# Reordering the second token group of a float32 language-model tower: sines inside the selection, biases as rows of the products, means as extra columns

## The chip, the cores and the metric

One NeuronCore of a Trainium2 chip runs the whole kernel in one launch. The metric is device time in microseconds, the median of several runs. The kernel before took 168.65 us (three runs, 168.17 to 169.03).

## The reference

Four sequences of 512 tokens, 64 channels, float32. Three layers follow each other:

```
# token layer
weighted = where(mask & ~eye, rel_dist, 0)
h = [atom_embed[ids], (weighted @ neighbor_embed[ids]) * w_rd] @ w1 + b1
h = silu(layernorm(h) * gamma + beta) @ w2 + b2
# attention layer, on x = layernorm(h)
ao     = gelu([x, pp] @ hop_w1 + hop_b1) @ hop_w2 + hop_b2       # 4 heads of 32 phases + 1 width
center = tanh(ao[:32]) * pi ; width = sigmoid(ao[32]) * 2 + 0.1
q      = cos/sin(pp + center + offsets), weighted by exp(-d^2 / 2 width^2), summed over 5 offsets
key_ph = tanh(x @ cpe_w + cpe_b) * pi ; values = x @ ve_w + ve_b
gate   = sigmoid(gelu(x @ sg_w1 + sg_b1) @ sg_w2 + sg_b2)
st_ph  = tanh(gelu([x, ctx/pos] @ ksk_w1 + ksk_b1) @ ksk_w2 + ksk_b2) * pi
combined = causal sums of (content, values * gate) against (cos, sin) of these phases
h = h + x + (layernorm(combined) * ln_g + ln_b) @ out_w + out_b
# experts, on x = layernorm(h): the best 2 of 8
h = h + sum over the 2 chosen experts of gelu(x @ W1[e] + b1[e]) @ W2[e] + b2[e]
```

## The kernel before, in words

**Tiles.** The four sequences form two groups of two. A group has 4 chunks of 128 tokens for each of its 2 sequences, so most tiles are 128 x 512, with tokens on the partitions, or channels of both sequences on them. PSUM is eight banks of 128 x 512 float32 (`bank[0]` to `bank[7]`), reused by hand.

**Stages.** Every engine has a function of the same name for each stage: `token(g)` (T), `project(g)` (P), `queries(g)` (Q), `chunks(g)` (C), `weights` (W) and `experts(g)` (X). Each is a generator, cut into parts by `yield`. `ORDER` (L83) is one list such as `P0 Q0 P1`; `follow` runs on each engine the next part of the named stage and group. The list is thus the program order of all engines together, each engine with its own parts of it; the instructions of an engine run strictly in that order. A part is written here as P1[2]: third part of `project` for group 1. Between engines there are only semaphores, `S[...]`.

**The parts that matter here.**

- T: TensorE multiplies by the centred second weight into bank 5 (L676), then by a two-column mean weight into bank 7 (L681). VectorE adds the bias to get h (L1160), takes the variance of ScalarE's squares, an inverse root in seven small operations (`rsqrt`, L1017), and writes x (L1168) and the means (L1170).
- P[0]: TensorE transposes x, ScalarE copies it out (L433); VectorE scans it (L1178). P[1]: the hop product (L703) and the position product (L704) into bank 1, the gate product (L707), two joint products of values, content and key phases (L712); ScalarE's two Gelus; VectorE adds the joints' biases (L1184). P[2]: the small width and gate products z (L727, L731), the storage product (L734, L736), joints 2 and 3; VectorE adds z's biases (L1190, L1192); ScalarE's third Gelu (L447) and the tanh of z. P[3]: centre products (L744), VectorE adds their bias into `t_c` (L1206), ScalarE takes the tanh in place (L458). P[4]: storage phase products (L756), their bias on VectorE (L1210), their tanh, and the gate's running sums (L762, L764, read at L1213).
- Q, on VectorE: Q[0] widths, Q[1] base angles (L1229), Q[2] sums over the five offsets, Q[3] an inverse root, the argument of the arctangent and the magnitude, Q[4] phases added to the angles (L1274), Q[5] the turn into range (L1280), Q[6] magnitude times sine and cosine (L1288), Q[7] sums over the heads into `feat` (L1295, L1299). ScalarE beside it: exponent, absolute value, key sines (L478), arctangent, rounding (L489), query sines (L494 to L500).
- C: C[0] TensorE transposes the keys (L783), C[1] the queries (L796), C[2] first scores, C[3] to C[5] a chunk each (scores L807 and L812, state, outputs L838 to L845), C[6] last outputs, C[7] variance and output products (L863, L869) and the output's means by two columns (L873), C[8] h3. On VectorE C[0] of group 0 also runs `weight_parts` (L1124), which centres the output weight and takes the low halves of expert weights.
- X[1]: VectorE's norm and split of the expert input; X[3]: selection of two experts, 16 small operations, ending in `mask_set`; X[4]: TensorE transposes the split with the mask (L926); from X[5] on one hidden product pair each (L944, L945), a Gelu (L574), and every second time four back products (L960).
- `spin_products(n, bank)` (L588) multiplies a constant tile n times and uses the result nowhere.

Two lines tell how an engine waits and why an order counts:

```
pe.wait_ge(S["q_sum"], 2 * g + 2)      # C[1]: query transposes
dve.wait_ge(S["gate_mm"], g + 1)       # P[4]: gate sums
```

After the group-1 query sums the list alternates C1 and X0, then X1 and X0, then X1 alone.

Of the kernel before, what the change touches and what calls it, by code (L numbers as in the profile page):

```python
# [45 lines left out]
P = 128  # L46
# [16 lines left out]
MASK_ROWS = 32  # L63
BIAS_AT, MASK_AT = D, D + MASK_ROWS
# [13 lines left out]
        ("hop2w_bd", P, 2 * H), ("hop_b2w", P, H)]  # L78
# [4 lines left out]
ORDER = ("T0 T0 T0 T0 T1 T1 T0 T0 T1 T0 T1 P0 P0 T1 P0 T1 Q0 P0 T1 W0 P0 Q0 P1 Q0 Q0 P1 Q0 Q0 Q0 Q0 P1 C0 P1 "  # L83
         "P1 C0 Q1 C0 Q1 C0 C0 Q1 C0 C0 Q1 C0 C0 X0 Q1 X0 Q1 X0 X0 C1 Q1 X0 X0 X0 X0 Q1 C1 X0 C1 X0 C1 X0 C1 X0 C1 X0 "
         "C1 X0 C1 X0 C1 X0 X1 X0 X0 X1 X0 X0 X1 X0 X0 X1 X0 X0 X1 X1 X1 X1 X1 X0 X1 X1 X1 X1 X1 X1 "
# [20 lines left out]
def tower(nc, ids, dist, mask, early, folded, late, ffn, mrows, out):  # L106
# [4 lines left out]
    with ExitStack() as ctx:  # L111
# [14 lines left out]
        def view(tile, table):  # L126
# [8 lines left out]
        w2c_bd = sb("w2c_bd", [P, P])  # L135
        w2_mean = sb("w2_mean", [P, NH_])
        b2c_rows = sb("b2c_rows", [P, D])
        shift = sb("shift", [P, 2])
        out_mean = sb("out_mean", [P, NH_])
# [8 lines left out]
        outw_g = sb("outw_g", [P, P])  # L148
# [85 lines left out]
        xp1 = [sb(f"xp1_{g}", [P, 8 * P], F32R) for g in range(NG)]  # L234
        xp2 = [sb(f"xp2_{g}", [P, 8 * P], F32R) for g in range(NG)]
# [20 lines left out]
            dist_masked h1_mm h1_copied h1t_mm h1_sq h1_norm hn_mm f_set h2_mm h_set h_mean_mm h_mean_set x_sq x_set  # L256
            trig_abs trig_set kang_set fold_mm fold_set fused_set
            xt_mm xt_set cx_set hop_mm hop_set sg_mm sg_set vk_mm vk_set z_mm zg_set tg_set ksk_mm ksk_set
# [7 lines left out]
        hid_bank = (0, 1, 3)  # L266
        x_bank = (0, 4)
# [15 lines left out]
        def b3(i):  # L283
            return bank[i][:, :].rearrange("p (t d) -> p t d", d=D)

# [104 lines left out]
        def _(act):  # L390
            def token(g):
# [19 lines left out]
                if g:  # L411
                    act.wait_ge(S["h_mean_mm"], g)
# [14 lines left out]
            def project(g):  # L427
# [14 lines left out]
                yield  # L442
# [4 lines left out]
                nc.scalar.activation(ksk_g[:, :], bank[2][:, :], ACT.Gelu,  # L447
                                     bias=ksk_bias[:, :]).then_inc(S["ksk_set"], 1)
                act.wait_ge(S["zg_set"], g + 1)
                nc.scalar.activation(tg[:, g], zg[:, g], ACT.Tanh, scale=0.5).then_inc(S["tg_set"], 1)  # L450
# [4 lines left out]
                for k in range(2):  # L455
                    act.wait_ge(S["center_set"], 2 * g + k + 1)
                    half = flat(t_c[:, g, 4 * k:4 * k + 4])
                    nc.scalar.activation(half, half, ACT.Tanh).then_inc(S["center_tanh"], 1)  # L458
                yield
                act.wait_ge(S["st_set"], g + 1)  # L460
# [124 lines left out]
        def _(pe):  # L585
# [14 lines left out]
            def token(g):  # L600
# [72 lines left out]
                if g:  # L673
                    pe.wait_ge(S["h_set"], g)
# [837 lines left out]
```

## Time and profile before

| | |
|---|---|
| median of three runs | 168.65 us (168.17 to 169.03) |
| the profiled execution | 169.19 us |
| its span in the trace | 167.4 us |
| mean granted TensorE clock | 0.959 |
| TensorE, VectorE, ScalarE busy | 149.0, 116.6, 81.8 us |
| the chain that ended last | TensorE 54%, VectorE 32%, ScalarE 6%, issue 6% |

The span is the time between the first and the last instruction in the trace; the rest of the execution lies around it. A busy TensorE need not be at its peak, since matmuls are pipelined and filling products count as busy. The granted clock is the share of 2.4 GHz: 1.00, or 0.50 for 1.2 GHz.

### The profile page before, as it was taken

How to read it: one execution, taken by the hardware profiler on the slowest of the kernel's cores; microseconds unless marked ns; L12 is line 12 of the kernel's file. 1: busy time of each engine (PE TensorE's matmuls, PEld its weight loads, DVE VectorE, ACT ScalarE, POOL GpSimd, SP SyncE). 2: the span in 40 equal slices, each digit the busy share in tenths (PEclk: the TensorE clock that was granted, in tenths of full speed). 3: DMA queues.
4: the chain of work that ended last, by engine and by line, in shares of the span. 5: the costliest groups of instructions: out<-in, count | busy, mean ns of one | idle time of the engine just before them, and what ended most of it. 6: DMA issues, size and time to landing. Idle time of an engine off the chain costs nothing.

```text
span 167.4 us, 2358 instructions
## 1 busy us (share of the span) xinstructions
PE 149.0 (89%) x806; PEld 88.4 (53%) x812; DVE 116.6 (70%) x344; ACT 81.8 (49%) x137; POOL 8.8 (5%) x38
## 2 busy tenths in 40 slices
PE   5899999999999988649699997786999999899991
PEld 1382565537693336429586752463665764553530
DVE  6999879975798989499859899993434788031202
ACT  3001151469389637962970232897224366545721
POOL 5403100140000000000000000000000000000000
PEclk9999999999999999956858999999999999999999
DMA  4899950300000000000000000000000000002011
GB/s 119 321 427 427 417 205 6 125 0 0 0 4 0 0 0 2 0 2 0 0 4 0 0 4 0 0 2 0 0 4 0 0 4 0 0 0 63 0 31 31
DMA packets 3778, 9.21 MB, mean 55 GB/s; under 512 B 2356, under 2 KB 2484, under 8 KB 3256
## 3 DMA queue, kind: packets, MB, share of 16 engines
q1 hardware_dynamic: 3768, 9.08, 14.6%
q8 instruction: 6, 0.10, 0.2%
q14 instruction: 4, 0.03, 0.1%
HBM read 8.55 MB, written 0.52 MB: 54 GB/s over the span
## 4 chain that ended last, share of the span: by engine, by line
PE 54%; DVE 32%; ACT 6%; issue 6%; POOL 0%; DVEq 0%; POOLq 0%; ACTq 0%
PE bank L960 9%; PE bank L944 6%; PE bank L646 5%; PE bank L945 4%; PE bank L624 3%; PE bank L807 2%; DVE invpos L1035 2%; PE bank L637 2%; DVE q_sc L1295 2%; DVE q_sc L1288 2%; PE bank L712 1%; PE bank L812 1%; PE bank L603 1%; PE bank L676 1%; DVE dist_sb L1274 1%
## 5 line engine op out<-in xcount | busy, mean ns | idle before, releaser
L590 PE MATMUL bank<-spin 128*128 128x512 bf16 x92 | 24.5, 398 | 5.2 <-POOL spin L328 2.0
L574 ACT ACTIVATE hid<-bank 128x512 f32<-128x512 f32 x32 | 17.9, 602 | 21.5 <-PE bank L945 21.4
L590 PEld LDWEIGHTS bank<-spin 128*128 128x128 bf16 x98 | 9.2, 104 | 15.8 <-issue 2.7
L960 PE MATMUL bank<-hid,ffn_sb 128*64 128x512 f32 x64 | 16.4, 612 | 0.0
L944 PE MATMUL bank<-xp,w1hi 128*128 128x512 f32 x32 | 14.6, 455 | 0.9 <-ACT xp L554 0.9
L1406 DVE TENSOR_TENSOR h<-bank,h 128x256 f32<-128x256 f32 (+1 forms) x5 | 1.8, 367 | 18.6 <-PE bank L971 12.8
L1313 DVE TENSOR_TENSOR dist_sb<-bank,fold_sb 128x256 f32<-128x256 f32 x16 | 6.0, 419 | 10.4 <-PE bank L812 9.8
L945 PE MATMUL bank<-xp,w1lo 128*128 128x512 f32 x32 | 12.6, 395 | 0.0
L944 PEld LDWEIGHTS bank<-xp,w1hi 128*128 128x128 f32 x32 | 6.0, 188 | 7.9 <-ACT hid L574 3.6
L646 PE MATMUL bank<-dist_sb,neigh 128*64 128x512 f32 x32 | 9.3, 699 | 0.0
L1085 DVE TENSOR_TENSOR dist_sb<-dist_sb,mask_in 128x1024 f32<-128x1024 f32 x8 | 9.2, 1218 | 0.0
L744 PE MATMUL bank<-late_sb,proj 128*128 128x256 f32 x16 | 5.7, 519 | 3.8 <-ACT proj L447 3.8
L807 PE MATMUL bank<-dist_sb 64*128 64x256 f32 x16 | 6.7, 502 | 1.5 <-ACT dist_sb L516 0.9
L395 ACT COPY neigh<-bank 128x512 f32<-128x512 f32 x2 | 1.2, 585 | 11.6 <-PE bank L624 11.6
L812 PE MATMUL bank<-dist_sb 64*128 64x128 f32 x32 | 6.8, 340 | 0.0
L1288 DVE TENSOR_TENSOR q_sc<-q_sc,mag 128x512 f32<-128x512 f32 x8 | 5.1, 687 | 2.4 <-ACT q_sc L497 2.4
L960 PEld LDWEIGHTS bank<-hid,ffn_sb 128*64 128x64 f32 x64 | 3.4, 135 | 6.3 <-issue 3.9
L744 PEld LDWEIGHTS bank<-late_sb,proj 128*128 128x128 f32 x16 | 3.8, 257 | 5.0 <-ACT proj L447 4.1
L945 PEld LDWEIGHTS bank<-xp,w1lo 128*128 128x128 f32 x32 | 6.1, 189 | 0.4
L646 PEld LDWEIGHTS bank<-dist_sb,neigh 128*64 128x64 f32 x32 | 3.1, 165 | 6.0 <-issue 4.9
L624 PEld LDWEIGHTS bank<-tables,onehot 100*128 100x128 f32 x32 | 5.4, 261 | 0.8 <-DVE tables L1056 0.8
L624 PE MATMUL bank<-tables,onehot 100*128 100x64 f32 x32 | 5.6, 348 | 0.0
(270 smaller groups left out, 318.3 us busy)
## 6 DMA issues: line engine op xcount, KB each, us to landing
dist_sb<-in_dist SPq DMA_DIRECT2D x4, 1024.0 KB, 11.2
mask_in<-in_mask SPq DMA_DIRECT2D x2, 512.0 KB, 8.1
fold_sb<-in_folded SPq DMA_DIRECT2D x1, 998.0 KB, 11.0
ffn_sb<-in_ffn SPq DMA_DIRECT2D x1, 816.0 KB, 17.4
late_sb<-in_late SPq DMA_DIRECT2D x1, 728.5 KB, 15.9
mask_in<-in_mrows SPq DMA_DIRECT2D x1, 512.0 KB, 3.1
out<-h SPq DMA_DIRECT2D x8, 64.0 KB, 1.7
early_sb<-in_early SPq DMA_DIRECT2D x1, 167.0 KB, 2.4
```

Of the source, the lines that this page charges most:

```text
L574: nc.scalar.activation(hid[:, at % HB], bank[hid_bank[at % 3]][:, :], ACT.Gelu).then_inc(S["hid_set"], 1)
L590: nc.tensor.matmul(bank[i][:, :], spin[:, 0:P], spin[:, :], start=True, stop=True)
L624: mm = nc.tensor.matmul(b3(5 if g == 0 else 7)[:, t], onehot[:, at:at + P], tables[:, D:2 * D], start=True, stop=True)
L646: mm = nc.tensor.matmul(rows(f), neigh[:, b, j], dist_sb[:, b, j], start=False, stop=(j == NC - 1), skip_group_check=True)
L744: mm = nc.tensor.matmul(bank[i][:, c * 256:(c + 1) * 256], hop_g[:, (2 * k + c) * P:(2 * k + c + 1) * P], K["hop2c_bd"], start=True, stop= ...
L807: nc.tensor.matmul(bank[4][:, 0:2 * P], k_t[lo, c, 0], q_t[lo, c].rearrange("p f i -> p (f i)"), start=True, stop=True).then_inc(S["s_mm"], 1)
L812: mm = nc.tensor.matmul(bank[5][:, f * P:(f + 1) * P], k_t[hi, c, f], q_t[hi, c, f], start=True, stop=True)
L944: nc.tensor.matmul(o, w1hi[:, e * HID:(e + 1) * HID], xp1[g][:, toks], start=True, stop=False)
L945: nc.tensor.matmul(o, w1lo[:, e * HID:(e + 1) * HID], xp2[g][:, toks], start=False, stop=True).then_inc(S["hid_mm"], 1)
L960: mm = nc.tensor.matmul(bank[2][j * D:(j + 1) * D, :], K["e_w2"][:, (e + j) * D:(e + j + 1) * D], hid[:, (at + j) % HB], start=False, stop ...
L1085: nc.vector.tensor_tensor(dist_sb[:, b, rows], dist_sb[:, b, rows], mask_sb[:, b, rows], ALU.mult).then_inc(S["dist_masked"], 1)
L1288: nc.vector.tensor_tensor(q3, q3, bc(mag[:, 16 * k:16 * k + 16], PH), ALU.mult).then_inc(S[done], 1)
```

## The change

1. **Order.** In the list, C0[0] (group 0's key transposes) moves ahead of Q0[4], and P1[1] behind Q0[5]: so the second group's joints on VectorE, its Gelus on ScalarE and its products on TensorE come after the first group's angles and sines. P1[2], P1[3] and P1[4] are interleaved with C0[2], C0[3] and C0[4]. Q1[0] to Q1[2] follow between C0[4] and C0[7]. Q1[3] comes after X0[2] instead of ahead of C0[7], C1[0] right after it, then Q1[4] and Q1[5], and only then X0[3], the selection, and Q1[6].
2. **Biases of group 1.** z, centre and storage phase biases come as an extra product at the head of each group of products: 64 rows of ones against 64 rows that hold the bias split into a high and a low float32r part (row 0 and row 32; the rest zero). ScalarE makes the high part and the ones in W, VectorE the low part (`bias_parts`) in P1[0]. ScalarE's tanh then reads the bank itself; VectorE's three additions go for group 1. Group 0 keeps them.
3. **Means as columns.** The token layer's and the output's mean weights become columns 129 and 130 of the same weight tile; chunks 0 and 1 go to bank 5, 2 and 3 to bank 7, and the separate mean products go. VectorE reads h, the scaled output and the means in two halves.
4. **Front of P[1].** The position product goes ahead of the wait for x; three filling products go. For group 1 the storage product and its Gelu move into P1[1], in bank 6.
5. **Weight parts** move from C0[0] to C0[1].
6. **Filling products** get new places and waits.

```
@@ ORDER
+ORDER = ("T0 T0 T0 T0 T1 T1 T0 T0 T1 T0 T1 P0 P0 T1 P0 T1 Q0 P0 T1 W0 P0 Q0 P1 Q0 Q0 C0 Q0 Q0 P1 Q0 Q0 C0 P1 "
+         "C0 P1 C0 P1 C0 Q1 C0 Q1 C0 Q1 C0 C0 X0 X0 X0 Q1 C1 Q1 Q1 X0 Q1 X0 X0 X0 X0 Q1 C1 X0 C1 X0 C1 X0 C1 "
...
@@ ScalarE, project
-                yield
+                if g == 0:
+                    yield
                 act.wait_ge(S["ksk_mm"], g + 1)
...
+                nc.scalar.activation(tg[:, g], bank[1][:, 0:40] if g else zg[:, g], ACT.Tanh, scale=0.5).then_inc(S["tg_set"], 1)
...
+                    nc.scalar.activation(half, bank[2 + k][:, :] if g else half, ACT.Tanh).then_inc(S["center_tanh"], 1)
@@ ScalarE, weights
+                nc.scalar.copy(b_rows[:, :], K["bias_rows"]).then_inc(S["b_hi"], 1)
+                nc.scalar.copy(b_ones[:, :], ones[0:2 * MASK_ROWS, 0:P]).then_inc(S["b_ones_set"], 1)
@@ TensorE, token
+                    mm = nc.tensor.matmul(with_mean(c // 2)[:, c % 2], f_t[:, c * P:(c + 1) * P], w2_ext[:, :],
...
-                    mm = nc.tensor.matmul(bank[7][:, c * NH_:(c + 1) * NH_], f_t[:, c * P:(c + 1) * P], w2_mean[:, :],
-                                          start=True, stop=True)
@@ TensorE, project
-                spin_products(3, 2)
+                nc.tensor.matmul(bank[1][:, :], K["hop1p"], K["pp_T"], start=True, stop=False)
                 pe.wait_ge(S["xt_set"], g + 1)
...
                 joint(0, 3)
                 joint(1, 0)
                 if g:
                     pe.wait_ge(S["h1_norm"], NG)
+                    storage()
+                    pe.wait_ge(S["h_mean_set"], NG)
+                    spin_products(4, 7)
+                    pe.wait_ge(S["phi_set"], 1)
+                    spin_products(5, 7)
+                    pe.wait_ge(S["th_sum"], 2)
+                    spin_products(5, 7)
+                    pe.wait_ge(S["th_set"], 2)
+                    spin_products(3, 7)
+                    last_joints()
+                    spin_products(3, 7)
+                    pe.wait_ge(S["cos_set"], 1)
+                    spin_products(3, 7)
+                    pe.wait_ge(S["cos_set"], 2)
+                    spin_products(4, 7)
+                yield
+                if g:
+                    pe.wait_ge(S["hop_set"], 2)
+                    pe.wait_ge(S["b_ones_set"], 1)
+                    pe.wait_ge(S["b_lo"], 1)
+                    nc.tensor.matmul(bank[1][:, 0:40], b_ones[:, :], b_rows[:, Z_AT:ST_AT], start=True, stop=False, skip_group_check=True)
...
                 def center(k, i):
+                    if g:
+                        nc.tensor.matmul(bank[i][:, :], b_ones[:, :],
+                                         b_rows[:, CENTER_AT:NB].unsqueeze(1).broadcast_to([2 * MASK_ROWS, 4, P]),
+                                         start=True, stop=False, skip_group_check=True)
@@ TensorE, chunks
+                if g == 0:
+                    pe.wait_ge(S["h_mean_set"], NG)
+                    spin_products(4, 2)
+                    pe.wait_ge(S["kph_abs_set"], 1)
+                    spin_products(5, 2)
+                    pe.wait_ge(S["k_feat"], 1)
+                    spin_products(5, 2)
...
                 yield
+                if g == 0:
+                    pe.wait_ge(S["ksk_set"], NG)
+                    pe.wait_ge(S["q_cos"], 2)
+                    spin_products(2, 7)
                 pe.wait_ge(S["q_sum"], 2 * g + 2)
@@ TensorE, experts, X0[3] and X0[5]
+                    spin_products(3, 2)
+                    pe.wait_ge(S["at_arg"], 2)
+                    spin_products(6, 2)
+                    pe.wait_ge(S["phi_set"], 2)
+                    spin_products(5, 2)
+                    pe.wait_ge(S["th_sum"], 4)
+                    spin_products(6, 2)
+                    pe.wait_ge(S["th_set"], 4)
                     spin_products(6, 2)
                     pe.wait_ge(S["first_best"], 1)
-                    spin_products(6, 2)
+                    spin_products(7, 2)
...
+                    spin_products(3, 2)
@@ VectorE
+            def bias_parts():
+                dve.wait_ge(S["b_hi"], 1)
+                low = slice(MASK_ROWS, 2 * MASK_ROWS)
+                nc.vector.tensor_tensor(b_rows[low, :], K["bias_rows"][low, :], b_rows[low, :].bitcast(F32),
+                                        ALU.subtract).then_inc(S["b_lo"], 1)
...
+                for n in range(2):
+                    dve.wait_ge(S["attn_mm"], 2 * g + n + 1)
+                    factor = st_c[:, 4 * n:4 * n + 4].rearrange("p (c f) -> p c f", f=NH_).unsqueeze(3).broadcast_to([P, 2, NH_, D])
+                    ins = nc.vector.tensor_tensor(comb[:, 2 * n:2 * n + 2], rows_of(n), factor, ALU.mult)
```

## Rows read from the trace of the kernel before

**Rows 1.** Windows, all engines: from:to, length, busy (instructions) by engine, granted clock:

```profile
98.00:110.00 12.00, 9.84 (x57) 5.62 (x57) 11.01 (x38) 7.12 (x13) 0.00 (x0) 1.00 0.01 1
115.00:128.00 13.00, 13.00 (x110) 7.74 (x110) 4.90 (x13) 3.96 (x7) 0.00 (x0) 1.00 0.01 1
```

**Rows 2.** Windows of TensorE alone, then granted clock, DMA share, GB/s:

```profile
35.10:37.21 2.11, 2.11 (x4) 1.00 0.00 0
39.83:41.70 1.87, 1.87 (x19) 1.00 0.00 0
45.45:47.22 1.77, 1.77 (x11) 1.00 0.00 0
48.03:49.95 1.92, 1.92 (x18) 1.00 0.00 0
73.51:78.65 5.14, 5.14 (x16) 0.50 0.01 2
78.70:82.05 3.35, 2.41 (x24) 1.00 0.00 0
82.05:88.85 6.80, 6.23 (x49) 0.50 0.01 2
115.92:116.35 0.43, 0.43 (x3) 1.00 0.00 0
122.03:123.71 1.68, 1.68 (x26) 1.00 0.04 10
```

**Rows 3.** Timeline, 45 to 60 us: start, length, engine, line, operation, tiles:

```profile
45.69 0.69 DVE L1160 TENSOR_TENSOR h<-bank,b2c_rows 128x512 f32<-128x512 f32 x1 [0.32 <-PE bank L676]
...
50.15 0.24 ACT L537 CAST eb<-ffn_sb 32x64 fp32r<-32x64 f32 x1
...
52.60 1.22 DVE L1229 TENSOR_TENSOR dist_sb<-dist_sb,half_turn 128x1024 f32<-128x1024 f32 x1
...
54.34 1.23 DVE L1178 TENSOR_TENSOR_SCAN proj<-ones,proj 128x512 f32<-128x512 f32 x1 [0.53 <-issue]
```

**Rows 4.** Timeline, 60 to 75 us, first group's query sines and sums:

```profile
67.27 1.28 ACT L497 ACT_TABLE_LOAD   x1
...
70.75 0.70 ACT L500 ACTIVATE q_sc<-thn,half_pi 128x512 f32<-128x512 f32 x1
...
74.09 0.49 DVE L1299 TENSOR_TENSOR feat<-q_sc 128x128 f32<-128x128 f32 x2
```

**Rows 5.** Windows of VectorE alone, one block of its order each:

```profile
56.21:58.48 2.27, 2.09 (x10) 1.00 0.00 0
75.60:78.22 2.62, 2.45 (x9) 0.50 0.00 0
80.43:81.78 1.35, 1.21 (x7) 1.00 0.00 0
91.13:95.28 4.15, 3.70 (x19) 1.00 0.00 0
95.28:98.55 3.27, 2.93 (x13) 1.00 0.00 0
98.55:100.64 2.09, 1.95 (x7) 1.00 0.04 8
100.64:104.58 3.94, 3.60 (x13) 1.00 0.00 0
105.78:109.49 3.71, 3.23 (x17) 1.00 0.00 0
109.49:114.37 4.88, 4.81 (x13) 1.00 0.01 2
```

**Rows 6.** Timeline, 90 to 100 us, ScalarE's square of the outputs:

```profile
93.16 0.60 ACT L527 ACTIVATE sq_c<-bank 128x512 f32<-128x512 f32 x1 [6.13 <-PE bank L845]
```

**Rows 7.** The chain that ended last, in order of time: start, length, what:

```profile
114.43 1.09 PE bank L796 x8
...
131.21 0.79 PE bank L873 x8
```

More of the change, by code:

```diff
@@ L679, in token @@
                 yield
-                for c in range(NC):
-                    mm = nc.tensor.matmul(bank[7][:, c * NH_:(c + 1) * NH_], f_t[:, c * P:(c + 1) * P], w2_mean[:, :],
-                                          start=True, stop=True)
-                mm.then_inc(S["h_mean_mm"], 1)
                 yield
@@ L713, in joint, with storage, last_joints @@
                                      stop=True).then_inc(S["vk_mm"], 1)
+                def storage():
+                    i = ksk_bank[g]
+                    nc.tensor.matmul(bank[i][:, :], K["ksk1x_bd"], x_t[:, :], start=True, stop=False)
+                    pe.wait_ge(S["cx_set"], g + 1)
+                    nc.tensor.matmul(bank[i][:, :], wk_bd[:, :], cx[:, :], start=False, stop=True).then_inc(S["ksk_mm"], 1)
+                def last_joints():
+                    for c, i in ((2, 3), (3, 0)):
+                        pe.wait_ge(S["vk_set"], NC * g + c - 1)
+                        joint(c, i)
                 joint(0, 3)
                 joint(1, 0)
+                if g:
+                    pe.wait_ge(S["h1_norm"], NG)
+                    storage()
[13 more added lines that the diff above has]
+                    spin_products(4, 7)
                 yield
                 if g:
[L719 to L724 removed]
+                    pe.wait_ge(S["hop_set"], 2)
+                    pe.wait_ge(S["b_ones_set"], 1)
+                    pe.wait_ge(S["b_lo"], 1)
+                    nc.tensor.matmul(bank[1][:, 0:40], b_ones[:, :], b_rows[:, Z_AT:ST_AT], start=True, stop=False, skip_group_check=True)
                 pe.wait_ge(S["hop_set"], g + 1)
@@ L868, in chunks @@
                 for c in range(NC):
-                    mm = nc.tensor.matmul(bank[5][:, c * P:(c + 1) * P], cc_t[:, c * P:(c + 1) * P], outw_g[:, :],
+                    mm = nc.tensor.matmul(with_mean(c // 2)[:, c % 2], cc_t[:, c * P:(c + 1) * P], outw_ext[:, :],
                                           start=True, stop=True)
-                mm.then_inc(S["attn_mm"], 1)
-                for c in range(NC):
-                    mm = nc.tensor.matmul(bank[7][:, c * NH_:(c + 1) * NH_], cc_t[:, c * P:(c + 1) * P], out_mean[:, :],
-                                          start=True, stop=True)
-                mm.then_inc(S["attn_mm"], 1)
+                    if c % 2:
+                        mm.then_inc(S["attn_mm"], 1)
                 yield
@@ L1168, in token @@
                 nc.vector.tensor_tensor(v8(x[:, g]), v8(h[:, g]), bc(st_r[:, :], D), ALU.mult).then_inc(S["x_set"], 1)
-                dve.wait_ge(S["h_mean_mm"], g + 1)
-                nc.vector.tensor_copy(h_mean[:, g], bank[7][:, 0:8]).then_inc(S["h_mean_set"], 1)
+                for n in range(2):
+                    ins = nc.vector.tensor_copy(h_mean[:, g, 4 * n:4 * n + 4].rearrange("p (c f) -> p c f", f=NH_), means_of(n))
+                ins.then_inc(S["h_mean_set"], 1)
                 yield
```

149 lines of the change are left out of this document (91 added, 58 removed).

## Prediction

> **What bounds the kernel now.** I read four views in this order: the page's forty slices, for where each engine is full and where TensorE's clock falls; the chain that ended last, for who sets the end; the timeline from 20 to 128 us, to lay each engine's order beside the others; windows over single blocks, for prices. A block below is written as in the order: P1[2] is the third part of project for the second group.
>
> From 114.43 on the chain is TensorE, without a gap until 143.5: it begins with the second group's query transposes [rows 7], and TensorE is busy 13.00 of 13 us there [rows 1]. What ends there is therefore set by when those transposes start, plus TensorE work taken out behind them. They start 0.06 us after the second group's query sums end on VectorE, at 114.37 [rows 5, 7]. Before that VectorE carries the chain: busy 11.01 of 12 us between 98 and 110 [rows 1]. So the question is how early VectorE ends the query sums of group 1. TensorE's half clock, 71.85 to 78.65 and 82.05 to 88.85 [rows 2], matters where VectorE waits for its products.
>
> **The change, step by step.** I keep the clock of the profiled execution.
>
> *Front end.* The first group's position product moves ahead of the copy of x it used to follow, and three filling products go. TensorE's transposes of x end about 34.25; position and x products (2.11 together [rows 2]) then end at 36.4 instead of 37.3: 0.9 early, on a stretch in which TensorE is the path to the second group's h. h starts at 45.69 now [rows 3], then at 44.8. Splitting h into two halves over two banks and the means into two copies costs some 0.07 and 0.1. The eight mean products that go cost what the second group's do, 0.79 [rows 7], beside VectorE work here: nothing.
>
> *Before the first queries.* ScalarE gets two casts, of 64x200 and 64x128. The nearest row is 32x64 at 0.24 [rows 3]; below I put 0.2 each, above 0.35 each, and take 0.5 in all. That delays the copy of x that starts the scan, which moves from 54.34 [rows 3] to 53.75 only. The new low part of the biases (0.3) runs while VectorE waits for that copy.
>
> *First group's queries.* At this point the second group's joints, 0.88, no longer stand in front of the angles, so th_sum starts near 63.0 instead of 64.35. The Gelus move behind the sines, so the table load between the absolute value and the first sine, 1.28 at 67.27, goes too. The last cosine, which ended at 71.45 (70.75 plus 0.70), ends at 68.75, and the query sums, which ended at 74.58 [rows 4], end at 71.9: 2.7 earlier. If the load still came, 1.3 of it would be lost. TensorE's new waits (for the turn, the sines, the last Gelu) hold up the last joints and the z products queued behind them, and nobody needs those before 74.5: VectorE stands in the query sums and the weight parts until then.
>
> The Trainium skill (ScalarE: Activation LUTs, "What ACT_TABLE_LOAD costs") budgets 2.66 us for each switch, a load of 1.28 and a drain of 1.38. The row has the load at 1.28, and the first sine starts 0.01 behind it, so the drain isn't in this trace. By the page's figure the sums would end 1.4 earlier still, near 70.5.
>
> *What is late next.* ScalarE needs a load and three Gelus after the last cosine (1.28 plus 1.9): to 72.0, and TensorE waits for the last of them, then runs two filling products: 72.45. From there its queue holds, at full clock and by the windows unless said [rows 2]: query transposes 1.09 [rows 7]; the 16 small z products 1.87; first scores 0.6; centre products 1.89 (the eight take 1.77 and a tail); a chunk 1.68; storage phase and gate products 1.92; a chunk 1.68; a chunk with three filling products 2.3; filling and last outputs 1.3: 14.4 us. The four bias products are new. By the nearest row, 512 columns of the same type at 0.43, they cost at most 1.7; below, a third of that and nothing if weights load beside others. I take 1.0. The outputs end at 72.45 + 15.4 = 87.8, against 93.1 now (the square that waits for them starts at 93.16 [rows 6]).
>
> The weight parts, 2.62 [rows 5], run from 71.9 to 74.5 beside the transposes; their cover is TensorE's z products, which VectorE awaits until 76. Were it gone they would cost 2.6. VectorE no longer adds the second group's biases (0.4 for z, 1.2 for centres, 0.4 for storage phases), but it idles while TensorE works: it waits at the gate sums until 82.5. What it saves there is not on the path.
>
> *From the outputs to the query sums of group 1.* Square, variance products and the first read take 2.2 now (93.1 to 95.28) and again: 89.95. VectorE has by then, after its second chunk at 84.1, the exponents' start 1.35, the base angles 1.22, the exponent sums 2.27 [rows 3, 5] and a masked chunk of 1.0: 89.95 too, a tie. Then, all on VectorE [rows 5]: variance to h3 and means 3.27, plus 0.1 for the halves, to 93.3; it waits 0.35 for ScalarE's square; norm and split 3.94, to 97.6; magnitude chain 4.15, now here, to 101.75; phases and their sums 2.09, to 103.85; a wait of 0.35 and the turn, 1.20 (between the rows ending 104.58 and starting 105.78), to 105.4; selection 3.71, to 109.1; products and sums 4.88, to 114.0. The sines need 3.4 after 104.9, so they end at 108.3, under the selection. Today's order has the same blocks and ends at 114.37. So five microseconds won at the outputs are nearly all spent again: today the magnitude chain fills VectorE's waits in the chunk stage, afterwards it stands in the open. What is left is 0.4.
>
> *Behind the transposes.* The second group's eight mean products, 0.79 at 131.21 [rows 7], go from a stretch where TensorE is the path; two more columns per product cost nothing visible. If ScalarE, which must do h3's square before its next Gelu, becomes late, none of it is kept; I take 0.8. The early scores and expert transposes (ready 7 us sooner) win nothing, because the mask ends at 109.1 and hidden products queue behind the query transposes anyway. The added 102 KB of biases ride in the fourth load, needed at 34.5 long after all loads have landed: nothing.
>
> Sum: 0.4 + 0.8 = 1.2. The profiled execution took 169.19 (span 167.40 and 1.79 around), so 168.0 in its terms; it lay 0.54 above the median of the three timed runs, 168.65, so I forecast 167.4 for the median. With all unknown costs at their good ends (biases 0.5, casts 0.3) it is 166.7; at their bad ends 168.2.
>
> **Rivals.**
>
> *The clock falls in the chunk stage (slower).* Now it fell once after TensorE had stood idle from 69.7, and once at 82.05, after a stretch in which it was busy 2.41 of 3.35 us, mostly with gate products of a few columns, and idle for 0.95 [rows 2]. The new queue puts z products of 8 and 2 columns and gate products of 8 and 6 in a row with scores. For it: such products alone preceded the second fall. Against: the new filling products leave no idle microsecond from 57 to 72.5, and small products from 48 to 50 fell between dense ones at full clock. Each half-clock stretch lasted 6.80 us [rows 2]; one of them over this full queue loses 3.4 us of work, and VectorE has no slack behind it: 167.4 + 3.4 = 170.8. It decides as soon as such a stretch begins between 73 and 84.
> The Trainium skill (TensorE: Matmul & The Clock Gate, "Part 1: The HAM clock gate") has half clock as the default that activity lifts; by that rule a queue kept full with tiny products may still count as quiet. The trace agrees in kind, with 0.50 granted at 82.05.
>
> *Everything is given back (no change).* The sines end only 0.8 under the selection and VectorE ties with TensorE at 89.95; half a microsecond late at two of these, or ScalarE eating the 0.8 around h3, and the transposes start at 114.4 to 115. For it: VectorE's work is the same. Against: the turn and sines have slack on both sides. Time: 168.65, give or take 0.4.
>
> *TensorE's stretch is shorter than its parts (much faster).* If weight loads run ahead and the bias products hide, VectorE's wait at the gate sums shrinks. VectorE's own work from 71.9 on adds up to some 37.4 us, so it could end at 109.3 at the earliest, 5 us before now. Half of the 4.7 us of waits gone gives 167.4 - 2.3 = 165.1. Against: the block prices are starts to starts at full clock, with overlap already in them.
>
> **How the numbers follow.** Forecast 0.46; given back 0.22; much faster 0.16; clock falls 0.16. From about 0.5% this kernel's measurement can tell a change: below 167.8 is faster, above 169.5 slower. Of the forecast four fifths lie below 167.8 (0.37), of the no-change case a small part (0.02): with the fast rival 0.55. Slower is the clock case: 0.16. The rest is 0.29. The likeliest case's own range is 166.7 to 168.2. Cutting half the fast rival and most of the clock case gives 165.2 to 169.8.
>
> **What would show it.** Right: the load before the first sines of group 0 gone and query sums end near 71.9; clock at 1.00 from 70 to 90; VectorE waiting for gate sums near 82; first outputs done near 88; second group's sines inside the selection; transposes near 114.0 and the stretch behind them 0.8 shorter. Wrong: a stretch at 0.50 between 73 and 90; sums of group 0 later than 73; the transposes before 113 or after 115, which means that a VectorE wait I placed is elsewhere.

## The result and the profile after

| | before | changed |
|---|---|---|
| median | 169.25 us (20 runs, 168.14 to 170.36) | 168.41 us (20 runs, 167.25 to 172.09) |
| the profiled execution | 169.19 us, span 167.4 | 168.35 us, span 166.6 |
| mean granted TensorE clock in it | 0.959 | 1.00 |
| TensorE, VectorE, ScalarE busy | 149.0, 116.6, 81.8 us | 152.4, 115.8, 79.7 us |

The ratio of changed to before is 0.9926, with an interval from 0.9898 to 0.9953. Of the 168.65 us on which the forecast was made that is 1.25 us, so 167.4. A few executions of the changed kernel (four of 20, near 172.0 us), and of most variants below, ran 3 to 9 us longer than their siblings; the ratios leave them out. The two profiled executions differ by 0.84 us, less than the ratio's 1.25.

The page of the changed kernel, three of its rows in forty slices. VectorE's thin place lies around the twentieth slice, and TensorE's granted clock does not fall in this execution (it fell twice in that of the kernel before [rows 2]).

```profile
PE   5899999899997799989999997896999999899991
...
DVE  6999879977699989993397899893424788131202
...
PEclk9999999999999999999999999999999999999999
```

ScalarE's timeline, 65 to 71 us, answers to [rows 4]: start, length, engine, line, operation. No table load stands before the sines, and the last cosine ends at 68.4, where it ended at 71.45. The load is now behind the sines, for the three Gelus.

```profile
64.96 0.63 ACT L521 ACTIVATE thn<-dist_sb 128x512 f32<-128x512 f32 x1 [0.21 <-DVE dist_sb L1375]
...
67.67 0.71 ACT L527 ACTIVATE q_sc<-thn,half_pi 128x512 f32<-128x512 f32 x1
68.40 1.28 ACT L452 ACT_TABLE_LOAD   x1
...
70.85 0.67 ACT L462 ACTIVATE proj<-bank,ksk_bias 128x512 f32<-128x512 f32 x1
```

VectorE's timeline, 71 to 92 us; in brackets its idle time and what ended it. The query sums end at 71.5, and then VectorE stands still five times for TensorE, 5.9 us in all, before the variance of the outputs (L1437).

```profile
71.01 0.49 DVE L1394 TENSOR_TENSOR feat<-q_sc 128x128 f32<-128x128 f32 x2
...
75.82 0.76 DVE L1408 TENSOR_TENSOR dist_sb<-bank,fold_sb 128x256 f32<-128x256 f32 x2 [0.90 <-PE bank L877]
...
79.22 0.76 DVE L1408 TENSOR_TENSOR dist_sb<-bank,fold_sb 128x256 f32<-128x256 f32 x2 [1.85 <-PE bank L882]
...
82.25 0.17 DVE L1308 COPY gsum<-bank 128x8 f32<-128x8 f32 x1 [2.08 <-PE bank L823]
82.88 0.76 DVE L1408 TENSOR_TENSOR dist_sb<-bank,fold_sb 128x256 f32<-128x256 f32 x2 [0.46 <-PE bank L882]
...
89.91 0.17 DVE L1437 TENSOR_SCALAR rs_v<-bank 128x8 f32<-128x8 f32 x1 [0.62 <-PE bank L933]
```

TensorE in windows, and its timeline. It is full, filling products included, from 57 to 70 us, stands idle for 0.81 before the first query transposes, and is full again from these to the last output of the first group (16.03 us, at full clock). Two groups of three filling products (L619) stand in front of the third and fourth outputs; in the chain that ended last they take 0.75 us each.

```profile
57.00:70.00 13.00, 13.00 (x50) 1.00 0.00 1
72.02:88.05 16.03, 16.03 (x146) 1.00 0.00 1
```

```profile
71.58 0.60 PE L619 MATMUL bank<-spin 128*128 128x512 bf16 x2 [0.81 <-ACT proj L462]
...
84.86 0.82 PE L619 MATMUL bank<-spin 128*128 128x512 bf16 x3
...
86.42 0.82 PE L619 MATMUL bank<-spin 128*128 128x512 bf16 x3
```

The chain that ended last, in order of time, answers to [rows 7]: the transposes start at 114.09 instead of 114.43. Behind them the chain now leaves TensorE once, for VectorE's scaled output and h3 (L1444, L1447), and then, as before, goes through ScalarE's copies (L593, L583) to the hidden products.

```profile
114.09 1.09 PE bank L866 x8
...
131.86 0.42 DVE dist_sb L1444
132.30 0.70 DVE h L1447
133.05 0.66 PE bank L960 x4
...
142.66 0.59 ACT proj L593
143.25 0.58 ACT xp L583
...
144.08 0.47 PE bank L1020
```

Of the 0.8 us by which the span is shorter, 0.34 is won at the transposes and 0.53 between them and the last block of hidden products (L1020, 144.08; before 144.95).

### The profile page after: what moved, and what is told of

Its sections match the earlier page's. It is cut to its first block, busy times and chain, and to the rows that moved or that the text cites. A ratio compares the mean times of both kernels' runs of the same rounds, so it can differ in the third digit from the quotient of the medians.

```text
span 166.6 us, 2404 instructions
## 1 busy us (share of the span) xinstructions
PE 152.4 (91%) x829; PEld 85.3 (51%) x829; DVE 115.8 (70%) x348; ACT 79.7 (48%) x137; POOL 8.8 (5%) x38
## 4 chain that ended last, share of the span: by engine, by line
PE 53%; DVE 32%; issue 6%; ACT 6%; POOL 0%; DVEq 0%; POOLq 0%; ACTq 0%
PE bank L1036 9%; PE bank L1020 5%; PE bank L1021 4%; PE bank L675 3%; PE bank L653 2%; DVE dist_sb L1161 2%; PE bank L619 2%; DVE invpos L1111 2%; PE bank L877 2%; DVE rs_v L1107 2%; PE bank L738 1%; PE bank L797 1%; PE bank L933 1%; PE bank L882 1%; PE bank L908 1%
## 5 line engine op out<-in xcount | busy, mean ns | idle before, releaser
L619 PE MATMUL bank<-spin 128*128 128x512 bf16 x143 | 36.4, 392 | 6.3 <-POOL spin L342 2.0
L619 PEld LDWEIGHTS bank<-spin 128*128 128x128 bf16 x143 | 13.0, 100 | 25.2 <-issue 4.1
L1020 PE MATMUL bank<-xp,w1hi 128*128 128x512 f32 x32 | 14.7, 458 | 0.4 <-ACT xp L583 0.4
L1508 DVE TENSOR_TENSOR h<-bank,h 128x256 f32<-128x256 f32 (+1 forms) x5 | 1.8, 367 | 18.2 <-PE bank L1047 12.3
L1020 PEld LDWEIGHTS bank<-xp,w1hi 128*128 128x128 f32 x32 | 6.0, 188 | 7.3 <-ACT hid L603 3.6
L882 PE MATMUL bank<-dist_sb 64*128 64x128 f32 x32 | 5.7, 297 | 0.0
L877 PE MATMUL bank<-dist_sb 64*128 64x256 f32 x16 | 5.5, 427 | 0.0
L1107 DVE TENSOR_REDUCE rs_v<-sq 128x8 f32<-128x520 f32 x6 | 4.1, 691 | 1.9 <-ACT sq L422 1.3
L738 PE MATMUL bank<-fold_sb,proj 128*128 128x320 f32 x16 | 5.2, 445 | 0.0
```

Source lines behind the costliest of these rows:

```text
L619: nc.tensor.matmul(bank[i][:, :], spin[:, 0:P], spin[:, :], start=True, stop=True)
L738: nc.tensor.matmul(bank[i][:, 0:VK], x_t[:, c * P:(c + 1) * P], K["vk_bd"], start=True, stop=True).then_inc(S["vk_mm"], 1)
L877: nc.tensor.matmul(bank[4][:, 0:2 * P], k_t[lo, c, 0], q_t[lo, c].rearrange("p f i -> p (f i)"), start=True, stop=True).then_inc(S["s_mm"], 1)
L882: mm = nc.tensor.matmul(bank[5][:, f * P:(f + 1) * P], k_t[hi, c, f], q_t[hi, c, f], start=True, stop=True)
L1020: nc.tensor.matmul(o, w1hi[:, e * HID:(e + 1) * HID], xp1[g][:, toks], start=True, stop=False)
L1107: link(nc.vector.tensor_reduce(rs_v[:, 0:8], squares[:, :, :], AX_X, ALU.add))
```

## Experiments

Each was run beside the kernel before on the same chip; ratios are to it. Edits are shown against the changed kernel, from experiment 10 on against the experiment in front; parts are left out where a line says so in words. In the first set the changed kernel, run again, had 0.9908 (0.9881 to 0.9935), median 168.13 us.

**1. The changed kernel again.** 

> The changed kernel itself, for a base on the same chip. My theory and every rival expect the ratio of the first measurement, 0.993, within its interval. The lists of runs so far have the changed kernel at a clock of 1.00 near 168.4 and at 0.979 near 167.4, and a few at 172.0; I expect the same three kinds of run again, the last by a half-clock stretch in the chunk stage.

It gave 0.9908, 1.6 us gained where the first measurement had 1.25; the intervals overlap.

**2. The second group's old order around the selection.**

```
 ORDER, from Q1[2] to Q1[6]
-Q1[2] C0[7] C0[8] X0[0] X0[1] X0[2] Q1[3] C1[0] Q1[4] Q1[5] X0[3] Q1[6]
+Q1[2] Q1[3] C0[7] C0[8] X0[0] Q1[4] X0[1] Q1[5] X0[2] X0[3] C1[0] Q1[6]
```

> The changed kernel with only the part of the list from Q1[2] to Q1[6] put back into the old order (magnitude chain ahead of the variance, angles and turn between the parts of the expert norm, selection after them). My theory: it is the same VectorE work, and the old order also covers two short waits of VectorE (0.3 for the square of h3, 0.3 for the rounding), so the second group's query transposes start between 113.3 and 114.2 instead of 114.09, and the kernel is 0 to 0.7 us faster than the changed one. Rival, that sines inside the selection are what wins: transposes 1 us or more later, kernel slower by 1 us or more.

Measured: 171.75 us, ratio 1.0109 (1.0072 to 1.0146), 3.4 us slower than the changed kernel. By the time alone the rival (1 us or more slower) would be right, but its reason is not what the trace shows. TensorE's timeline of it:

```profile
93.59 1.25 PE L619 MATMUL bank<-spin 128*128 128x512 bf16 x5 [2.04 <-DVE rs_v L1437]
96.51 1.11 PE L960 MATMUL bank<-fold_sb,h 128*128 128x128 f32 x4 [1.67 <-DVE h L1447]
...
100.26 5.26 PE L619 MATMUL bank<-spin 128*128 128x512 bf16 x12
...
106.24 7.29 PE L619 MATMUL bank<-spin 128*128 128x512 bf16 x33
...
117.15 1.04 PE L866 MATMUL bank<-fold_sb,feat 128*128 128x128 f32 x8
```

and VectorE's last query sums in the same execution:

```profile
112.09 0.49 DVE L1394 TENSOR_TENSOR feat<-q_sc 128x128 f32<-128x128 f32 x2
```

VectorE ended the sums at 112.6, 1.4 earlier than in the changed kernel. But TensorE, idle at 91.6 and 94.8 because h3 comes later in this order, was granted 0.50 from about 95.3 to 105.3, and then ran 33 filling products in a row (7.3 us), all behind waits that had long been met. The query transposes stood behind these, and behind 3.8 us of transposes and hidden products that the fillers had held up, and started at 117.15, 4.6 us after their data.

**3. The same order, with TensorE's fillers fitted to it.**

```
 X0[0]
-spin_products(4, 2)
+spin_products(13, 2)
 pe.wait_ge(S["var_read"], 1)
-spin_products(5, 2)
+spin_products(12, 2)
 X0[3]: 3, at_arg, 6, phi_set, 5, th_sum, 6, th_set, 6, first_best, 7
-> 8, first_best, 7
```

> The order before the change from the third part of queries for the second group on (magnitude chain ahead of the variance, phases and turn among the first group's expert parts) with TensorE's fillers fitted to it: 13 and 12 instead of 4 and 5 at the first expert part, 8 instead of 3, 6, 5, 6, 6 behind the split rows' transposes. Theory 1, the earlier trial of this order was slow by TensorE's idle time, its half clock and fillers behind waits already met, and not by VectorE: with fitted fillers the clock stays at 1.00 past 90, the query sums end near 112.5 and the query transposes start there: 1 to 1.5 us faster than the changed kernel, ratio to the kernel before 0.982 to 0.987. Theory 2, the order itself is what costs (late h3 makes something else late): 1 us or more slower than the changed kernel, ratio over 0.998, at full clock. Theory 3, the clock falls in any such order: ratio near 1.01 and 0.50 granted near 95 again.

Measured: 168.15 us, ratio 0.9894 (0.9843 to 0.9945). The interval holds both the changed kernel's ratio and the upper end of the expectation. Its profiled execution took 167.32 us, with the clock at 1.00 from 57 us on:

```profile
112.51 0.49 DVE L1386 TENSOR_TENSOR feat<-q_sc 128x128 f32<-128x128 f32 x2
```

```profile
113.06 1.09 PE L866 MATMUL bank<-fold_sb,feat 128*128 128x128 f32 x8 [1.11 <-DVE feat L1386]
```

The transposes start 1.0 earlier than in the changed kernel's trace and the execution is 1.0 shorter. So the order was not what made experiment 2 slow: same order, full clock, 3.6 us less by the ratios. That the old order is the faster one for VectorE stands in two traces (sums 1.4 earlier in experiment 2, transposes 1.0 earlier here) and not in the ratio.

**4. Without the new fillers.**

```
 P1[1] and C0[1], TensorE
-spin_products(4, 7) ... (5, 7) (5, 7) (3, 7) (3, 7) (3, 7) (4, 7) ... (2, 7)
 the waits between them stay
```

> The changed kernel without the 29 filling products that it has between the second group's storage product and the first group's query transposes (4, 5, 5, 3, 3, 3, 4 and 2; the waits stay). Theory 1, the fillers carry the full clock into the chunk stage: TensorE idles most of 57 to 71, is granted 0.50 from about 70 for 6.8 us, as before the change, and as VectorE has only 0.6 us of slack at the variance read, 3.4 us of lost work cost some 2.8: ratio to the kernel before near 1.008, 2.8 us slower than the changed kernel. Theory 2, the clock is full again by the time that the queue matters, or the stretch falls on work that is covered: within 0.5 us of the changed kernel, ratio 0.990 to 0.995.

Measured: 174.82 us, ratio 1.0285 (1.0247 to 1.0323), 6.4 us slower than the changed kernel. TensorE in windows:

```profile
64.00:68.00 4.00, 1.32 (x4) 1.00 0.00 0
...
70.00:75.00 5.00, 2.98 (x13) 0.50 0.00 2
...
80.00:85.00 5.00, 5.00 (x15) 0.50 0.00 0
85.00:86.00 1.00, 1.00 (x17) 0.90 0.00 0
```

VectorE, where it waits for the gate sums and for the variance:

```profile
88.31 0.17 DVE L1300 COPY gsum<-bank 128x8 f32<-128x8 f32 x1 [2.06 <-PE bank L816]
...
95.96 0.17 DVE L1429 TENSOR_SCALAR rs_v<-bank 128x8 f32<-128x8 f32 x1 [0.62 <-PE bank L925]
```

TensorE idled for 6.8 of the 8 us between 64 and 72, was granted 0.50 from about 68.1, and stayed there to 85.2, through most of the chunk stage. Gate sums and variance came 6.1 later. The mechanism of theory 1 is shown; the loss is over twice its 2.8 us: one stretch of 6.8 was assumed, and it lasted 17. What the change gains hangs on these 29 products.

**5. Each bias product twice.**

```
+nc.tensor.matmul(bank[1][:, 0:40], b_ones[:, :], b_rows[:, Z_AT:ST_AT], start=True, ...)
 nc.tensor.matmul(bank[1][:, 0:40], b_ones[:, :], b_rows[:, Z_AT:ST_AT], start=True, ...)
 and so for both centre products and the storage product
```

> The changed kernel with each of the four bias products of the second group issued twice in a row (the second starts the bank anew, so the result is the same). Theory 1, TensorE sets the stretch from 72 to 88 and the bias products stand in it, 0.2, 0.5, 0.45 and 0.3 in the trace: outputs end 1.4 later, VectorE's wait at the variance read (0.62) grows by as much and all behind comes 1.4 later: ratio to the kernel before 0.999 or 1.000 where the changed kernel has 0.991. Theory 2, products of eight rows hide under the weight loads beside them, or the waits take it: within 0.3 us of the changed kernel, ratio 0.991 to 0.993.

Measured: 168.9 us, ratio 0.9946 (0.9919 to 0.9974); its profiled execution 169.26, 0.9 over the changed kernel's. Each pair took from its first start to the start behind it 0.33, 0.74, 0.66 and 0.43, together 2.16, where the single products take 1.46. TensorE and VectorE of it:

```profile
75.78 0.58 PE L794 MATMUL bank<-xp 64*128 64x512 f32 x1
76.20 0.39 PE L797 MATMUL bank<-xp 64*128 64x512 f32 x1
76.52 1.13 PE L801 MATMUL bank<-late_sb,proj 128*128 128x256 f32 x4
```

```profile
83.19 0.17 DVE L1315 COPY gsum<-bank 128x8 f32<-128x8 f32 x1 [2.20 <-PE bank L830]
...
90.84 0.17 DVE L1444 TENSOR_SCALAR rs_v<-bank 128x8 f32<-128x8 f32 x1 [0.63 <-PE bank L940]
```

Gate sums and variance are 0.9 later than in the changed kernel, 0.23 of which is there at the query transposes (72.25) already: the other 0.70 is just what the pairs added, and the whole is 0.6 (by the ratios) to 0.9 longer. The ratios' intervals overlap, so this rests on the trace: TensorE sets this stretch, the bias products stand in it, and VectorE had no slack to give. That is theory 1, at half its size, since the second product of a pair adds half of what a single one takes.

**6. The separate mean products back.**

```
+for c in range(NC):
+    nc.tensor.matmul(bank[6][:, c * NH_:(c + 1) * NH_], cc_t[...], out_mean, start=True, stop=True)
```

> The changed kernel with the eight small mean products of the output put back behind the output products, into an unused bank, result unused. In the profiles the part behind the second group's query transposes became 0.5 us shorter, not 0.8. My theory: TensorE won 0.87 at the output products and lost about 0.3 of it at h3 and at ScalarE's copy behind h3's square; so this kernel is 0.5 us slower than the changed one. Rival, that the two extra columns and the halves cost nothing and all of 0.8 is there: 0.8 slower. Rival, that none of it is on the path: same.

Measured: 168.1 us, ratio 0.9921 (0.9892 to 0.9949), 0.1% over the changed kernel of the same set: below what this can tell. Its profiled execution lost the clock where the first rival said:

```profile
76.10:82.90 6.80, 6.80 (x22) 0.51 0.01 2
```

That execution took 172.59 us, over 4 more than its median.

**7. Gelus ahead of the sines, by the list.**

```
 ORDER, from C0[0] to P1[1]
-C0[0] Q0[4] Q0[5] P1[1]
+P1[1] Q0[4] Q0[5] C0[0]
```

> The changed kernel with the second group's products and Gelus put back ahead of the first group's rounding and sines (and the key transposes behind them), all else as changed. My theory: the table load and the joints stand in front of the sines again, first query sums end 2 us or more later (near 73.8), TensorE's stretch starts there, and since nothing behind it has slack the kernel is 1.5 to 2.2 us slower than the changed one. Rival, that VectorE's slack of 2 us at the gate sums takes it: within 0.5 us.

Measured: 171.85 us, ratio 1.0164 (1.0118 to 1.021), 4.3 us slower than the changed kernel. VectorE's sums ended 2.8 later. The rest was again TensorE: 4.0 us idle, 0.50 granted from 62.7 to 69.5, and 24 fillers in a row that ended at 75.65, behind the sums.

**8. Gelus ahead of the sines on ScalarE alone, fillers added.**

```
 ScalarE, Q0[3]
 nc.scalar.activation(wscr[:, 3], wscr[:, 2], ACT.Arctan)
+hop, gate and storage Gelu of group 1
 TensorE, P1[1]: 4, 5, 5, 3, 3, 3, 4  ->  4, 5, 12, 6, 6, 3, 4
```

> The changed kernel with the second group's three Gelus right behind the first group's arctangent on ScalarE, so that the first group's sines need their table load again; no other engine's order is touched, and TensorE gets 13 filling products more (12, 6, 6 instead of 5, 3, 3) so that it does not idle meanwhile. Theory 1, the Gelus ahead delay the evening by 2.1 and the load adds 1.3: last cosine 71.8 instead of 68.4, query sums 74.9, query transposes 2.9 later than 72.0, and as TensorE's stretch and VectorE's chain follow without slack, 2.9 us slower than the changed kernel, at full clock: ratio near 1.008. Theory 2, VectorE's waits in the chunk stage take part of it: 1 to 2 us slower, ratio 0.997 to 1.003. Theory 3, the earlier trial's clock fall comes back and was most of its loss: ratio over 1.012 with 0.50 granted between 62 and 80.

Measured: 174.25 us, ratio 1.0246 (1.0189 to 1.0303). ScalarE and TensorE of it:

```profile
61.56 1.28 ACT L445 ACT_TABLE_LOAD   x1
...
68.34 1.28 ACT L533 ACT_TABLE_LOAD   x1
69.63 0.63 ACT L533 ACTIVATE q_sc<-dist_sb 128x512 f32<-128x512 f32 x1
```

```profile
75.71 1.09 PE L875 MATMUL bank<-fold_sb,feat 128*128 128x128 f32 x8 [1.01 <-DVE feat L1403]
```

From the first phase sums on VectorE to the end of its query sums it took 12.3 us, and 8.8 in the changed kernel: 3.5 more, 2.0 of it in front of the turn and 1.3 the load (2.1 and 1.3 expected). The query transposes followed, 3.7 later in the trace, or 3.0 with the 0.7 taken off by which this execution is later from the start. So the Gelus' new place brings the chunk stage forward by about 3.0 us in this trace. But 13 more fillers did not hold the clock either: TensorE idled 1.0 before 75.71 and was granted 0.50 from about 79.6 to 86.4. All six executions had a mean clock of 0.96 to 0.98, so the loss of 5.7 us against the changed kernel isn't the move alone, and how much of it is can't be read from the ratio.

**9. VectorE's waits filled.**

```
 ORDER, from P1[3] to X0[0]
-P1[3] C0[3] P1[4] C0[4] Q1[0] C0[5] Q1[1] C0[6] Q1[2] C0[7] C0[8] X0[0]
+P1[3] Q1[0] C0[3] P1[4] C0[4] Q1[1] C0[5] Q1[2] C0[6] C0[7] C0[8] X0[0]
 VectorE, P1[4]:  + base angles of group 1, ahead of the gate sums
 TensorE, third and fourth outputs:  - spin_products(3, 2)
```

> The changed kernel with VectorE's waits in the chunk stage filled: the second group's exponents start before the first masked chunk, its base angles before the gate sums, its exponent sums before the wait for the last outputs, and the two groups of 3 fillers ahead of the third and fourth outputs are left out. Theory 1, the five microseconds won at the outputs were spent because VectorE stood still for 7.9 us between 75 and 90 and TensorE's two filler groups lay on the path: outputs end 1.5 earlier (86.5), the variance is read near 88.4 instead of 89.9 with VectorE waiting for it about 1, and all behind follows, query transposes near 112.5: 1.5 us faster than the changed kernel, ratio 0.982 to 0.985. Theory 2, ScalarE's extra table loads (tanh, exp, tanh, sine in place of tanh, exp, sine) or the missing fillers' clock eat it: no faster than the changed kernel, with a table load or 0.50 granted to be seen between 78 and 95.

Measured: 166.98 us, ratio 0.9819 (0.9784 to 0.9854), at the edge of the expected 0.982 to 0.985. Two edits were made together, and neither was run alone. In the changed kernel's trace the two filler groups take 1.5 us of TensorE's path to the outputs; without them, and with VectorE's order kept, the variance could be read only 0.62 earlier, which is VectorE's wait there. With VectorE's order alone changed, the outputs would come no earlier. So the 1.5 us need both: TensorE's path shortened, and VectorE's ready work laid into its waits, where the changed kernel did it later, in the open. The split is read from that trace and not shown by a run.

**10. The magnitude chain ahead of the variance as well.**

```
 ORDER
-C0[6] C0[7] C0[8] X0[0] X0[1] X0[2] Q1[3] C1[0]
+C0[6] Q1[3] C0[7] C0[8] X0[0] X0[1] X0[2] C1[0]
 TensorE, X0[0]: 9 and 13 fillers instead of 4 and 5; X0[3]: 5 instead of 3 and 6
```

> As the kernel with the waits filled, and the second group's magnitude chain ahead of the variance read, so that VectorE doesn't wait there at all (fillers 9 and 13 instead of 4 and 5 at the first expert part, 5 instead of 3 and 6 behind the split rows' transposes). Theory 1, only VectorE's sum of work counts from 82 on: exponent sums end 87.4, magnitude 91.5, h3 94.9, query sums 111.3: 2.7 us faster than the changed kernel, ratio 0.974 to 0.978. Theory 2, h3 2.5 us later leaves TensorE idle or at half clock, and it counts: slower than the version with the magnitude chain behind, ratio above 0.985, with 0.50 granted between 90 and 105. Theory 3, behind the query transposes ScalarE or the h3 of the second group caps the gain: between the two.

Measured: 166.68 us, ratio 0.9836 (0.9807 to 0.9864); expected 0.974 to 0.978. Not different from experiment 9. VectorE's row says where the second step went:

```profile
102.35 1.30 DVE L1378 SCALAR_TENSOR_TENSOR dist_sb<-thn,dist_sb 128x512 f32<-128x512 f32 x2 [1.49 <-ACT thn L516]
```

The turn waits 1.49 for ScalarE's rounding, which stands behind copies of the split rows and the keys:

```profile
99.58 1.07 ACT L578 CAST xp<-bank 128x512 fp32r<-128x512 f32 x2 [4.19 <-PE bank L980]
100.54 1.09 ACT L538 COPY dist_sb<-bank 128x512 f32<-128x512 f32 x2
101.49 1.36 ACT L516 ACTIVATE thn<-dist_sb,even 128x512 f32<-128x512 f32 x2
```

A wait taken away on VectorE came back on ScalarE. Theory 3 had ScalarE as the cap, but behind the query transposes and not here.

**11. Sines ahead of those copies.**

```
-X0[1] X0[2] C1[0] Q1[4] Q1[5] X0[3]
+X0[1] Q1[4] Q1[5] X0[2] C1[0] X0[3]
 TensorE, X0[3]: 5, phi_set, 5, th_sum, 6, th_set, 6, first_best, 7
 -> 3, th_sum, 6, th_set, 8, first_best, 6
```

> The version with the waits filled and the magnitude chain first, with the second group's phases and turn and sines ahead of ScalarE's copies of the split rows and of the second group's keys (in that version VectorE waited 1.49 us for ScalarE before the turn, 0.26 in the changed kernel), fillers 3, 6, 8, 6 in the fourth expert part. Theory 1, VectorE's chain is still what sets the query transposes: the turn starts 1.2 earlier, the selection and the query sums too, transposes near 111.0 instead of 112.2: 1.2 us faster than that version, ratio to the kernel before near 0.976. Theory 2, the copies now come late and the expert products behind them, or the hidden products of the first group, set the end: no faster than that version, ratio 0.983.

Measured: 166.01 us, ratio 0.9781 (0.9739 to 0.9824), 0.9 us below experiment 10 by the ratios, whose intervals overlap; expected 1.2. The wait before the turn is 0.26 again.

**12. With TensorE's idle time before the last Gelu filled.**

```
 pe.wait_ge(S["cos_set"], 2)
-spin_products(4, 7)
+spin_products(7, 7)
```

> The version with the sines ahead of the copies, with 7 instead of 4 filling products behind the first group's last cosine, which fill TensorE's idle 0.8 us before the last Gelu ends. In the profiled execution of that version, and in those of two others, TensorE was granted 0.50 from 75 or 76 on, after that idle stretch and 2 us of products of 8 and 2 columns, and the execution was 3.5 to 4 us longer than its siblings. Theory 1, the idle stretch is the trigger: no execution of this kernel has it, all lie within 165 to 166.5, ratio near 0.978. Theory 2, the small products alone are the trigger: the fall still comes in some executions, at 75 to 76, with times near 169.7. Theory 3, with the idle stretch gone another execution's clock falls elsewhere, at a place to be read.

Measured: 165.55 us (165.08 to 169.78), ratio 0.9772 (0.9728 to 0.9817), not different from experiment 11. It is 3.9 us below the kernel before by the ratio and 2.3 to 2.6 below the changed kernel (by its two ratios). One of six executions took 169.78 us at a mean clock of 0.98, so theory 1 is out; whether its clock fell at 75 or elsewhere isn't known, as the trace is of another execution. VectorE and the transposes in the profiled execution (165.25 us):

```profile
93.40 0.69 DVE L1448 TENSOR_TENSOR h<-dist_sb,x 128x512 f32<-128x512 f32 x1
...
101.14 1.30 DVE L1376 SCALAR_TENSOR_TENSOR dist_sb<-thn,dist_sb 128x512 f32<-128x512 f32 x2 [0.26 <-ACT thn L516]
```

```profile
111.01 1.09 PE L866 MATMUL bank<-fold_sb,feat 128*128 128x128 f32 x8 [1.59 <-DVE feat L1395]
```

h3 comes 1.1 later than in the changed kernel (92.30) and the query transposes 3.1 earlier; 0.9 of that was already there at 62 us, before any of the edits. The span is 3.1 shorter.

## Why the prediction was right, step by step

*The number:* right, with some luck. The forecast added 0.4 at the query transposes and 0.8 behind them. The two profiled executions, which have the forecast's terms, gave 0.34 and 0.53, 168.35 us where 168.0 was forecast. The ratio's 1.25 agrees with the forecast's 1.2, but 0.4 of it is in no trace, and the second measurement had 1.6.

*Front end and first queries:* right. h at 44.72 (44.8 forecast), the scan at 53.49 (53.75), the first phase sums at 62.69 (63.0). The two casts delay ScalarE by 0.56 (0.5). These are readings of one trace; no run has this part of the change alone.

*The table load:* right. It is gone from the sines' path, and the query sums end at 71.50 (71.9). What the Trainium skill says of it (ScalarE: Activation LUTs, "What ACT_TABLE_LOAD costs"), 1.28 and a drain of 1.38, agrees with the traces in the load alone: in experiment 8 the load begins at 68.34 and the sine at 69.63, 0.01 after its end. The sums' end lies 0.4 below the forecast from the row, and 1.0 above the 70.5 that the page's figure gave.

*TensorE's stretch:* right at the sum, by two errors that nearly cancel. It starts at 72.02, 0.4 before the forecast's 72.45, and takes 16.0 us against 15.4, so it ends at 88.05 against 87.8. The bias products were put at 1.0 and took 0.21, 0.51, 0.43 and 0.31 from start to start, 1.46 in all; experiment 5's trace shows what is added there paid in full. Letting VectorE add those biases in one of its waits would have been the other choice; it wasn't tried.

*The tie at the variance:* the read is right within 0.1, at 89.91 (89.95). It was no tie: VectorE was ready 0.62 earlier, and TensorE and ScalarE set it.

*From there to the query sums:* right. h3's means, norm, magnitude, phases, turn and selection end at 93.4, 97.6, 101.8, 103.9, 105.4 and 109.1, each within 0.1 of the forecast, and the transposes start at 114.09 (114.0; before 114.43). The claim that 5 us won at the outputs are spent again because VectorE's work stands in the open was the core of the forecast. Experiments 9 to 12 bear it out from the other side: with the same work laid into the waits, and two filler groups (1.5 us) off TensorE's path, 2.3 us or more come out. The forecast had these fillers in its sum and did not ask what they were worth. Nor did it see that the magnitude chain's new place, and the sines inside the selection, lose about 1 us before the transposes (experiments 2 and 3, by trace).

*Behind the transposes:* right in size, weak in proof. The mean products' removal shortens the stretch from the transposes to the hidden products (L1020, 144.08; before 144.95) by 0.5, not by 0.8, since TensorE's transposes of x then wait for VectorE's h3 (chain above). Experiment 6 can't tell even that from nothing.

*The clock rival:* its condition was incomplete. In the changed kernel's profiled execution the clock stayed at 1.00; four of its 20 executions took 172.0 to 172.1 at a mean clock of 0.980, some 3.6 over the others at 1.00, close to the 3.4 forecast, but none of the four was traced. Experiment 6's profiled execution shows the very fall that was named, 76.1 to 82.9, at over 4 us instead of 3.4. The forecast's reading of the kernel before was wrong in part: of the 2.41 busy us ahead of the second fall only about 1.0 was gate products, and eight transposes of 128 columns took as much, so tiny products did not precede that fall alone. The argument against the rival wasn't quite so either: the new fillers leave 0.81 us idle before 71.58. Still they were worth more than the forecast gave them: without them the kernel is 4.8 us slower than before (1.0285), where the rival had 2.2. The Trainium skill (TensorE: Matmul & The Clock Gate, "Part 1: The HAM clock gate") has the half clock as the state that TensorE falls back to without activity; experiment 4 agrees, with TensorE idle for most of 64 to 68 and 0.50 granted from 68.1.

*Where the first explanation fell:* experiment 2 was to show that the new place of the magnitude chain costs VectorE 0 to 0.7. Its time said nothing of that, because TensorE's fillers had been laid out for another order; its trace had VectorE's sums 1.4 earlier. Experiment 3 repaired the fillers.

## What to carry to other kernels

When an engine that waits is ahead of a stretch in which it alone works, first count its idle time and the work that is ready, and the filling products on the producer's path. Here a faster producer brought 0.3 us at the query transposes until that work was moved into the waits and the fillers were taken off. An order and its filling products are one thing: when one of them moved here, fillers behind waits already met became pure delay (experiment 2), and idle time without fillers cost the clock for most of a stage (experiment 4). After each removed wait, look on the engine that feeds the same instruction for what is queued in front.

## What the hardware showed beyond that

The half clock does not fall at the same place in every execution of one program. In profiled executions of experiments 6, 9 and 11 it lay over the chunk stage; in those of experiments 10 and 12 over the loads at the start, where the DMA engines are busy throughout (share 1.01) and TensorE loses nothing that counts; those executions were among the shortest. TensorE's windows of experiment 12 and, below, of experiment 11:

```profile
9.45:16.25 6.80, 6.80 (x24) 0.54 1.01 424
```

```profile
71.00:72.00 1.00, 0.23 (x2) 1.00 0.02 8
...
75.90:82.60 6.70, 6.70 (x20) 0.50 0.01 2
```

The lists of times fit: of the changed kernel's 20 executions five, at a mean clock of 0.979, took 167.25 to 167.40 us, eleven at 1.00 took 168.00 to 168.71, and four at 0.980 took 172.01 to 172.09. Nearly the same mean clock stood for the shortest and the longest. What decides where it falls, and why everything up to 62 us is 0.9 earlier in the traces with the early stretch, stays open. In experiment 4 the half clock lasted 17 us at one go, with TensorE busy 13.1 of them, so pricing a fall at one stretch of 6.8 us can be far too low.
